# A gated cross-attention block: loads in order of need, other rows a step on, six steps peeled

## The reference

```python
# x (32, 56, 128), ctx (32, 1500, 128), all fp32; 16 heads of depth 8; 160 experts, 8 chosen
q = layernorm(x) @ Wq.T + bq;  k = ctx @ Wk.T + bk;  v = ctx @ Wv.T + bv
attn = softmax(q k^T / sqrt(8));  x = x + tanh(g_xattn) * ((attn v) @ Wo.T + bo)
y = layernorm(x)
probs = sigmoid(y @ router_w.T + expert_bias);  top 8, normalised, times 2.5
routed = sum over experts of combine_e * silu(y @ w_gate_e.T) @ w_down_e.T
shared = silu(y @ w_gate_shared.T) @ w_down_shared.T
out = x + tanh(g_ffn) * (routed + shared)
```

## Time and profile before

| | us |
|---|---|
| median of 3 runs (1124.66 to 1126.08) | 1125.85 |
| the profiled execution | 1124.83 |
| its span | 1123.2 |
| TensorE busy | 1068.0 (95%) |
| VectorE busy | 963.5 (86%) |
| ScalarE busy | 847.6 (75%) |
| GpSimd busy | 591.7 (53%) |

### The profile page before, as it was taken

The page is one execution under the profiler, slowest core; times in us unless marked ns, Lnnn a source line. Parts: engine busy times, 40 slices in busy tenths (PEclk is TensorE's granted clock), DMA queues, the critical chain, the costliest instruction groups (busy, mean ns, idle before and its releaser), DMA issues.

```text
span 1123.2 us, 37415 instructions
## 1 busy us (share of the span) xinstructions
PE 1068.0 (95%) x12142; PEld 708.1 (63%) x12142; DVE 963.5 (86%) x1699; ACT 847.6 (75%) x1817; POOL 591.7 (53%) x984
## 2 busy tenths in 40 slices
PE   2799999999999999999999999998999999999998
PEld 1366777777777777777777777654455555555554
DVE  4678888888888888888888888578999999999998
ACT  3476777777777777777777776687888888888887
POOL 5798887887888888788888886320000000000000
PEclk9799999999999999999999999999999999999999
DMA  8778777577577576676676652482788778777873
GB/s 159 158 166 214 145 178 179 123 184 170 133 186 170 131 186 162 142 185 152 152 185 142 150 132 67 110 207 97 229 228 226 226 236 237 229 229 227 230 237 118
DMA packets 229501, 197.12 MB, mean 175 GB/s; under 512 B 161039, under 2 KB 207263, under 8 KB 229462
## 3 DMA queue, kind: packets, MB, share of 16 engines
q1 hardware_dynamic: 218036, 173.22, 61.8%
q0 software_dynamic: 9200, 21.85, 6.9%
q10 hardware_dynamic: 2226, 1.56, 0.7%
HBM read 109.96 MB, written 12.55 MB: 109 GB/s over the span
## 4 chain that ended last, share of the span: by engine, by line
PE 75%; DVE 12%; issue 4%; SPq 3%; ACT 2%; DMA 2%; DVEq 0%; POOL 0%; ACTq 0%
PE bank L1550 15%; PE bank L1540 15%; PE bank L1343 12%; PE bank L1377 11%; PE bank L1358 10%; DVE part_max L1030 6%; PE bank L1413 5%; PE bank L1401 4%; DVE rec L1169 2%; PE bank L1457 1%; SPq L369 1%; DMA ctx_in<-in_ctx_dram 1%; SPq L405 1%; DVE o_raw L1044 1%; DVE kparts L1160 1%
## 5 line engine op out<-in xcount | busy, mean ns | idle before, releaser
L800 ACT ACTIVATE p_exp<-bank 125x448 f32<-125x448 f32 x768 | 400.1, 544 | 183.9 <-PE bank L1358 182.9
L1030 DVE TENSOR_REDUCE part_max<-bank 128x1 f32<-128x500 f32 x672 | 420.1, 671 | 62.0 <-PE bank L1377 61.5
L1358 PE MATMUL bank<-q_st,k_stk 97*125 97x224 f16 x1536 | 272.6, 261 | 2.5 <-ACT p_exp L800 1.9
L1377 PE MATMUL bank<-kparts,q_blk 128*128 128x500 f16 x672 | 255.8, 384 | 17.5 <-DVE part_max L1030 13.2
L1358 PEld LDWEIGHTS bank<-q_st,k_stk 97*125 97x125 f16 x1536 | 195.9, 138 | 66.2 <-ACT p_exp L800 13.1
L867 ACT ACTIVATE ctT<-bank 128x448 f32<-128x448 f32 x320 | 174.2, 545 | 40.9 <-DVE v_sb L1203 9.8
L1210 DVE TENSOR_TENSOR ctT<-v_sb,ctT 128x448 f16<-128x448 f32 (+1 forms) x324 | 200.4, 619 | 0.2
L1550 PE MATMUL bank<-ctT,w_ring 128*128 128x448 f16 x816 | 198.9, 352 | 0.1
L874 ACT ACTIVATE ctT<-v_sb 128x448 f16<-128x448 f32 x320 | 182.2, 569 | 7.0 <-DVE v_sb L1203 6.9
L1343 PE MATMUL bank<-p_exp,v_sb 125*25 125x168 f32 (+1 forms) x6144 | 186.2, 262 | 0.4 <-ACT p_exp L800 0.4
L1343 PEld LDWEIGHTS bank<-p_exp,v_sb 125*25 125x25 f32 x6144 | 142.1, 103 | 42.6 <-ACT p_exp L800 0.5
(11 more groups left out here) (193 smaller groups left out, 1376.3 us busy)
## 6 DMA issues: line engine op xcount, KB each, us to landing
k_stk<-kparts SPq DMA_DIRECT2D x384, 93.8 KB, 4.1
v_sb<-c_scratch SPq DMA_DIRECT2D x68, 448.0 KB, 4.3
k_stk<-c_scratch SPq DMA_DIRECT2D x68, 448.0 KB, 4.3
ctx_in<-in_ctx_dram SPq DMA_DIRECT2D x30, 672.0 KB
w_scratch<-w_out POOLq DMA_DIRECT2D x80, 128.0 KB, 3.2
w_in<-in_L_ffn_w_gate_dram POOLq DMA_DIRECT2D x80, 64.0 KB, 3.7
w_in<-in_L_ffn_w_down_dram POOLq DMA_DIRECT2D x80, 64.0 KB, 4.1
v_sb<-c_scratch SPq DMA_DIRECT2D x8, 336.0 KB, 3.8
```

Of the source, the lines that this page charges most:

```text
L800: act.activation(p_exp[0:KP, j % PR, f * 448:(f + 1) * 448], ST[f][0:KP, 0:448], ACT.Exp).then_inc(exp_done, 1)
L1030: v.reduce_max(part_max[:, i // NCH, i % NCH:i % NCH + 1], SM[i % NSM][:, 0:CK], axis=AX.X).then_inc(sm_maxed, 1)
L1358: last = pe.matmul(ST[f][0:KP, (g % 2) * GC:(g % 2 + 1) * GC], k_stk[0:97, u, g, j * KP:(j + 1) * KP], q_st[0:97, u, g, :, :].rearrange("p ...
L1377: pe.matmul(SM[i % NSM][:, 0:CK], rows, kparts[:, u, 0, c * CK:(c + 1) * CK], start=True, stop=True).then_inc(sm_done, 1)
```

## The change

Loads: SP issues x of FIRST and the three chunks of context 0; ACT issues the four weights behind the padding rows. Context 1 and x of REST move to SP: behind the three transposing loads of batch 0, with the stacking copies of the first queries between and behind them. GpSimd's memsets of den_spread and k_stk come ahead of the first split. In the start the product of the first queries comes ahead of the first key chunk, on TensorE and ScalarE.

REST rows: centred in three parts in step 1, squared at (1, 10), root at (1, 11), scaled at (2, 1); tokens at (2, 3), (2, 7), (2, 11), their products a place later. They go through KB instead of banks 0 and 1. So the tokens wait for the keys' remainder before them, and the key chunks at (2, 6), (2, 10) and (3, 2) wait for the queries' remainder (KEYS_BEHIND). Six steps instead of four are written out; the 12 stacking copies come four at a time behind steps 3, 4 and 5, and GpSimd waits for them ahead of step 6. `queries_free` waits for chunk 0 alone.

```diff
-    VAR_REST_AT, RSTD_REST_AT, SCALE_REST_AT = (1, 1), (1, 2), (1, 3)
-    TOKENS_REST_AT = {(1, 5): (1, 3), (1, 8): (3, 4)}
-    Q_REST_AT = {(1, 6): (1, 3), (1, 9): (3, 4)}
-    Q_HI_REST_AT = {(1, 7): (1, 3), (1, 10): (3, 4)}
-    Q_LO_REST_AT = {(1, 8): (1, 3), (1, 11): (3, 4)}
+    CENTRE_REST_AT, SQUARE_REST_AT = {(1, 5): 1, (1, 7): 2, (1, 9): 3}, (1, 10)
+    VAR_REST_AT, RSTD_REST_AT, SCALE_REST_AT = (1, 11), (2, 0), (2, 1)
+    TOKENS_REST_AT = {(2, 3): (1, 2), (2, 7): (2, 3), (2, 11): (3, 4)}
+    Q_REST_AT = {(2, 4): (1, 2), (2, 8): (2, 3), (3, 0): (3, 4)}
+    Q_HI_REST_AT = {(2, 4): (1, 2), (2, 8): (2, 3), (3, 0): (3, 4)}
+    Q_LO_REST_AT = {(2, 5): (1, 2), (2, 9): (2, 3), (3, 1): (3, 4)}
+    KEYS_BEHIND = {(2, 6): 2, (2, 10): 3, (3, 2): 4}
-        REST_ROWS_AT = {2: (0, 2, 1)}
-        QB = [bank[0], bank[0], bank[1], bank[0]]
+        REST_ROWS_AT = {3: (0,), 4: (2,), 5: (1,)}
+        QB = [bank[0], KB, KB, KB]
@@ attention
-            for s in range(first, 4):
+            for s in range(first, 6):
-            with eng.Fori(2, loop_to // 2) as h:
+            with eng.Fori(3, loop_to // 2) as h:
@@ SP
-            load_chunk(0)
-            for n, w in enumerate((Wq, Wk, Wv, Wo)):
-                sp.dma_start(w_raw[:, n, :], w).then_inc(weights_in, 16)
-            for c in range(1, NCH):
+            for c in range(NCH):
                 load_chunk(c)
...
                 transpose_ctx(0, c, c + 1, None)
+            load_rows(sp, ctx_here[1], ctx_in[0:KP, 1, :, :], ctx[1].rearrange("(p j) c -> p j c", j=KT))
+            stack_queries(0, 1, (0,), q_rows)
+            load_x(sp, *REST, x_rest)
+            stack_queries(0, 1, (1,), q_rows)
+            transpose_chunks((0, 0), (0,))
             load_ctx((0, 0))
-            stack_queries(0, 1, (0, 1), q_rows)
-            transpose_chunks((0, 0), (0,))
             stack_queries(0, 1, (2,), q_rows)
@@ GpSimd
-            attention(pool, body, B - 2, {2: first_pairs, 3: add_constant, 4: all_rows})
+            attention(pool, body, B - 2, {2: first_pairs, 3: add_constant, 6: all_rows})
@@ ACT
+            for n, w in enumerate((Wq, Wk, Wv, Wo)):
+                act.dma_start(w_raw[:, n, :], w).then_inc(weights_in, 16)
-            load_x(act, *REST, x_rest)
-            load_rows(act, ctx_here[1], ctx_in[0:KP, 1, :, :], ctx[1].rearrange("(p j) c -> p j c", j=KT))
...
-            first_keys(0)
             act.wait_ge(bqs_made, 1)
             queries(0, 1)
+            first_keys(0)
-            square_rest()
@@ DVE
-            dve.wait_ge(x_rest, 32)
-            centre(*REST)
+            def centre_rest(c):
+                dve.wait_ge(x_rest, 32)
+                centre(c * PPC, (c + 1) * PPC)
@@ PE
-                        pe.wait_ge(q_lo_done, 2 if c == 3 else 1)
+                        pe.wait_ge(k_lo_done, 2 * NCH + c)
...
+                        if isinstance(step[0], int) and (b, k) in KEYS_BEHIND:
+                            pe.wait_ge(q_lo_done, KEYS_BEHIND[(b, k)])
```

More of the change, by code:

```diff
@@ L276, in attention @@
                 body((s // 2, s % 2))
-            if 4 in before:
-                before[4]()
-            with eng.Fori(2, loop_to // 2) as h:
+            if 6 in before:
+                before[6]()
+            with eng.Fori(3, loop_to // 2) as h:
                 body((h, 0))
@@ L600, in add_constant @@
                 pool.wait_ge(constant_made, 1)
-                pool.wait_ge(ln_sub, 2)
+                pool.wait_ge(ln_sub, NTC)
                 pool.tensor_tensor(xt[:, :, :], xt[:, :, :], bo_b[:, :].unsqueeze(1).to_broadcast([PT, NP, D]),
                                    ALU.add).then_inc(pre_done, 1)
-            pool.wait_ge(pad_here, 32)
-            for c in range(NCH):
-                split_ctx((0, 0), c)
             const(pool.memset(den_spread[:, :], 0.0))
@@ L615, in _ @@
             assert made[0] == K_ONES
+            pool.wait_ge(pad_here, 32)
+            for c in range(NCH):
+                split_ctx((0, 0), c)
             const(pool.memset(v_sb[:, :, :, 0:4, 3 * d:VW], 1.0))
@@ L736, in square_rest @@
             def square_rest():
-                act.wait_ge(ln_sub, 2)
+                act.wait_ge(ln_sub, NTC)
                 for p in range(*REST):
@@ L805, in body @@
                             values(back(step, 1), k // TPC)
-                    aside(step, k, (VAR_REST_AT, lambda: root(2, *REST)), (SCALE_REST_AT, scale_rest),
+                    aside(step, k, (SQUARE_REST_AT, square_rest), (VAR_REST_AT, lambda: root(2, *REST)), (SCALE_REST_AT, scale_rest),
                           *((at, lambda c=c: query_tokens(*c)) for at, c in TOKENS_REST_AT.items()),
@@ L1052, in body @@
                                         negate=True).then_inc(neg_made, 1)
-                    aside(step, k, (VAR_REST_AT, variance_rest), (RSTD_REST_AT, rstd_rest),
+                    aside(step, k, *((at, lambda c=c: centre_rest(c)) for at, c in CENTRE_REST_AT.items()),
+                          (VAR_REST_AT, variance_rest), (RSTD_REST_AT, rstd_rest),
                           *((at, lambda c=c: queries(*c)) for at, c in Q_LO_REST_AT.items()),
@@ L1301, in _ @@
             query_tokens(1, 0, 1)
+            queries(0, 1)
             first_keys(0)
-            queries(0, 1)
             first_keys(1)
@@ L1319, in queries_free @@
             def queries_free():
-                pe.wait_ge(q_hi_done, NTC)
-                pe.wait_ge(q_lo_done, NTC)
+                pe.wait_ge(q_hi_done, 1)
+                pe.wait_ge(q_lo_done, 1)
                 pe.wait_ge(k_ones, 32)
```

## The result

The changed kernel takes 1141.52 us (median of 4 runs, 1140.9 to 1142.35) against 1125.26 for the kernel before in runs on the same chip: ratio 1.015, interval 1.0129 to 1.0171. It is slower, as forecast, but by 16.3 us where 8.8 were forecast, and it lies above the range. The profiled execution after took 1142.35 us with a span of 1140.8; before, the span was 1123.2. The two spans differ by 17.6.

What follows compares the result with a forecast made beforehand. TensorE was taken as the bound from the third attention step on. Terms -0.3 + 6.3 + 1.5 - 1.0 + 3.2 = +9.7, less 0.9 for gaps, gave +8.8: 1134.7 us on the median, range 1124.5 to 1141.

Steps and rivals of the forecast that it cites:

- part 3: ScalarE between steps 1 and 2: late squares and scaling delay keys and gates, losing 6.6 of 6.9 us.
- part 6: Spread stacking copies gain 1.0 us in step 4; GpSimd's wait for the last ones loses 3.2 in step 7.
- part 4: Steps 2 and 3: other rows through the keys' bank add TensorE work and waits, losing 6.3 us.
- Part 1: Start: loads in order of need bring the first maxima product to 17.5 from 27.05, gaining 9.5 us.
- Part 2: Step 1: later context 1 and added centring lose 2.7 us; the step ends at 43.9, 6.9 early.
- part 5: Step 2: TensorE's stall at k = 3 brings 3 us more at half clock, losing 1.5 us.
- the gaps: Step 2: TensorE's existing gaps may be covered by the new waits, taking 0.9 us off the loss.
- A: Start's gain survives to step 2's end, TensorE fills gaps, GpSimd is not late: 1122 to 1125 us, chance 0.14.
- B: Steps lose as forecast, but GpSimd's wait for the stacked rows is hidden: +5.6, 1131.5 us, chance 0.27.
- C: Step 1: transpose of (1, 0) waits behind x and context 1, landing at 29: +12.7, 1138.6 us, chance 0.13.

Runs made afterwards that it cites:

- e4: Changed kernel's loads, start and peeling, but other rows centred, squared, scaled and tokenised in step 1 through banks 0 and 1, stacked behind steps 2 to 4: 1117.32 us.
- e6: e1 with the other rows centred in one piece at (1, 2) and squared at (1, 3): 1127.87 us.
- e7: e6 with the other rows' root and scaling also early, at (1, 5) and (1, 6): 1129.66 us.
- e11: e1 with 92 unused products filling TensorE's gap ahead of its wait at (2, 3): 1133.35 us.
- e3: Kernel before with only six steps written out and the other rows' stacking copies spread behind steps 2, 3 and 4: 1122.71 us.
- e1: Changed kernel with the last eight stacking copies issued behind step 4, none behind step 5: 1133.73 us.
- e2: e1 with the gates and shared weights taken ahead of the scaling at (2, 1): 1132.63 us.
- e9: e4 with the sixteen small DMA issues for the output weights' rows moved to (1, 0) to (1, 3): 1119.75 us.

## Why the prediction was right and wrong

The sign, the places of the loss and what released each wait were right; the sum was short by half. Two terms failed by their size, the chain of part 3 (by 3.0 us) and the late rows of part 6 (by 4.8), and part 4 was 1.8 short. By its own steps:

**Part 1, the start.** The first maxima ran at 20.18, not 17.5, outside the part's own 16 to 19. The step that failed is "the query product ahead of the first key chunk costs that chunk nothing". The product was to end at 12.7 and began at 13.32, and from there TensorE's own work, the query product and nine key products to 18.55, sets the time, and then the evacuation and the remainder, 1.5 us. The last chunk was to land at 15.5, its 12.2 and 3.8 less 0.5 for a lighter queue that no row showed; it landed by 16.5 and was not what TensorE waited for. **Part 2** gave much of that back: step 1 ended at 45.0, forecast 43.9, inside its bounds. That it lost time at all was right, but not that it must: in e4 the same work in one piece at (1, 2), with more behind it, ends the step no later.

**Part 3 failed by size.** k = 5 of step 2 was to start at 62.7, 0.3 us before the old place. It starts at 66.56, 3.6 behind it. The path is the one that was written down, and its links are late by a little more from one to the next:

| link | forecast | measured | added there |
|---|---|---|---|
| last centring ends | 42.8 | 44.16 | 1.4 |
| keys' evacuation ends | 47.1 | 49.53 | 1.0 |
| gates' copies end | 55.7 | 58.06 | -0.1 |
| keys' remainder ends | 58.9 | 61.91 | 0.6 |
| k = 5 starts | 62.7 | 66.56 | 0.9 |

The first is in the main one operation: the scaling of four sums (L955) took 1.53 us, where its two fellows of this step took 0.63 and 0.20. It ran while GpSimd issued its DMAs (last section). The second is 1.04 us in which ScalarE stands behind the squares: its queue issues four copies of the output weights' rows there (L790, 46.14 to 48.80), and the evacuation starts behind the last. In the kernel before it did so too: its idle time of 1.62 us at 52.69 is put down to issue. The prediction had this row, took the squares for what sets the time of the evacuation, and did not ask what the issue in it was. The fourth is 0.57 us between the copies' end and VectorE's first operation behind them, which the sum did not have, and VectorE's constant term, 1.44 for 1.2; the maxima were 0.2 shorter. The last, 0.9, is the slow clock, which the prediction had in part 5, so part 3 proper is 3.0 short, its own lower bound. That the late centring and squares are the chief cost was found by e6 (5.9 us). The scaling's place is not: e7, which takes it away, ends step 2 no earlier than e6.

**Part 4 was right in its waits and 1.8 us too small.** From k = 5 to the end of step 3 the kernel after takes 38.7 us against 31.5, 7.2 more; part 4 less the gaps had 5.4 for it (the slow clock of part 5 lies ahead of k = 5). The waits were 1.51 and 0.94, forecast 1.5 and 0.9, and 0.51 to 0.72 for the queries' remainder, forecast 0.4. TensorE was busy 34.26 us there, 30.89 before: 3.4 more, where 2.6 had been summed. And it stood for 4.4 us, 0.6 before: the gaps that were to cover 0.9 us were not there. It stayed inside the part's bounds.

**Part 5, the clock.** The gap of 5.2 us at (2, 3) was there (4 to 5 forecast), and the clock was at 0.50 to about 65.8. By the last link of part 3 it costs 0.9 us, and by e11 0.8 and by e6 up to 2.0, where 1.5 was taken. What was forgotten is the second place: the same happens behind the wait in step 7, with 2.4 us. The Trainium skill's page "TensorE: Matmul & The Clock Gate" (Part 1: The HAM clock gate) says that an idle engine is halved and restored only after sustained work; both gaps agree, 0.52 over 62 to 66 and 0.51 over 176 to 182, each some 4 us near half speed. The prediction had the rule and used it once. The clock was at 0.50 in the kernel after from 42 to 54 as well, where e4 had 1.00 throughout.

**Part 6 failed by size in its second term.** The gain was 1.8 us over steps 4 to 6, forecast 1.0; e3 shows the 1.1 of step 4 alone. The loss was 8.0 in steps 7 to 9, forecast 3.2. Its wait was too short and the clock was left out. GpSimd began 155.96 - 146.39 = 9.6 us behind the end of step 5, forecast 8.5 (145.4 against 136.9). The 1.1 is the issues: 1.9 us from the first to the fourth had been taken from the eight q_hi copies (5.02), but the four that come last are those of q_lo, and these took 3.7 us after (3.68) and in the kernel before as well:

```profile
82.54 3.65 SPq L369 DMA_DIRECT2D q_stk<-q_lo  x4
```

TensorE wanted q_st 26.4 us behind the end of step 5 (172.8 against 146.39), where the forecast had 26.8 (163.7 against 136.9), since step 6 was 0.5 shorter. With both, and 0.1 for GpSimd's step, the wait is 3.2 + 1.1 + 0.4 + 0.1 = 4.8, measured 4.96. The 2.4 us of slow clock come on top, and 1.1 us more in steps 8 and 9. That GpSimd could not shorten its step was right: 21.6 us, as before.

**The rivals.** A is out: step 2 ends at 82.17, not before 71. B is out as the result, yet e1 is its world, and it came out at 9.4 us, not 5.6: the 3.8 are about what parts 3 to 5 together were short (4.2). C is out by its landing, though its 12.7 was nearest to the 16.3; that nearness is luck. The range left out the case in which the one mechanism was right and two terms were off the same way; its upper end came from C alone, and the bounds of parts 3 (3 worse) and 6 (5 for 3.2) together would have carried it to 1139.5, with the clock in step 7 to 1142.

What the start is worth, then: 5.4 us by e4 over e3, with the other rows' work fitted into step 1. The change spent about 14 us of step 2 to have the other rows' work a step later, and 8 us on copies that came a step too late.

## To carry to other kernels

When work is moved from a stage that waits into one that is full, price it as the chain that it makes on each engine, with the DMA issues that now stand beside it, and not as its busy time. A resource borrowed from a running pipeline (here the bank of the keys) is charged with the wait for its owner at each loan, so look first for one that is idle, as banks 0 and 1 were in step 1. A stall of some 5 us on TensorE in a full stage was followed here by some 4 us near half speed, 0.8 to 2.0 us of time in step 2 and 2.4 in step 7: count it at every place where it happens.

## What the runs showed that had not been expected

Operations of VectorE on a handful of elements were at times many times slower than their fellows, and mostly the trace shows what GpSimd did beside them. In the start, L963 on 112x4 is the same work in all eleven kernels with the new loads. It took 0.17 us in e7, where it fell between two operations of GpSimd, and 0.30 to 1.10 us in the ten others, where it began beside one and ended 0.01 to 0.03 us behind it. In the kernel after:

```profile
8.07 1.16 POOL L567 TENSOR_TENSOR ctx_parts<-ctx_in,ctx_parts 128x512 f16<-128x512 f32 x1
8.15 1.10 DVE L963 TENSOR_SCALAR stat<-stat 112x4 f32<-112x4 f32 x1
```

So does L1021 in e2 (1.18 us, ending at 57.60, GpSimd's operation at 57.52). The hold of 1.5 us at the third centring is less clear. GpSimd was issuing its pairs of weight loads from 37.42 to 44.37, without a break, and L955 took 1.53 us at 41.90 but 0.20 at 38.00, both beside these issues. It came back in all six kernels with the third centring at (1, 9): in five the same small operation, begun between 41.35 and 41.99, took 1.52 or 1.53, and in e1 the next one, L956, begun at 42.20, took 2.24 instead of 0.69. No run moved GpSimd's issues, so this one stays a correlation.

DMA issues hold up their engine's own instructions: four of 0.63 to 0.66 us on ScalarE, 46.14 to 48.80, were followed by an evacuation that started at 48.85, 1.04 us after the engine's last square, with its product made since 41.2. Moving such issues away did not pay in e4's setting (e9).

Step 1 hides more than its busy shares say. It took in the centring, squares, scaling and three sets of tokens (e4) and ended no later than in the kernel after, where of all this only the centring and the first squares stand in it.
